# Query feature steps of four heads and 256 tokens in place of two heads and 512 tokens

## The reference

```python
def _fourier_kernel(x, proj_mat):
    p = jnp.einsum('blhd,dm->blhm', x, proj_mat) / math.sqrt(D_HEAD)
    return jnp.concatenate([jnp.cos(p), jnp.sin(p)], axis=-1) / math.sqrt(D_KMAP)
q = (x2 @ wq + bq).reshape(B, L, N_HEAD, D_HEAD)      # 16 heads of 16
k, v = ...                                            # the same with wk, wv
qp = _fourier_kernel(q, proj_mat)                     # 128 cosines, 128 sines a head
kp = _fourier_kernel(k, proj_mat)
kv = jnp.einsum('blhm,blhd->bhmd', kp, v)
attn = jnp.einsum('blhm,bhmd->blhd', qp, kv)
x = x + attn.reshape(B, L, D_MODEL) @ wo + bo
# then: layer norm, relu(x2 @ w1 + b1) @ w2 + b2 added
```

## Time and profile before

| | |
|---|---|
| median of three timed runs | 2267.7 us (2265.14 to 2273.48) |
| the profiled execution, its span from first to last instruction | 2298.2 us, 30.5 us (1.3%) over that median |
| mean granted TensorE clock | 0.942 of full speed |
| PE busy | 1940.0 us (84%) |
| DVE busy | 1682.0 us (73%) |
| ACT busy | 1255.4 us (55%) |
| POOL busy | 1225.0 us (53%) |
| query steps (qf) of batch 0, 1, 2, 3, from the first turns to the last attend's end | 98 to 154, 313 to 368, 527 to 581, 740 to 794 us |

### The profile page before, as it was taken

How to read it: one execution, slowest core, us unless ns; L and a number is a source line. 1 busy time by engine, 2 the same in 40 slices (tenths; PEclk the granted TensorE clock), 3 DMA queues, 4 the chain that set the end, 5 groups by cost and what they waited for, 6 DMA issues and landing times. The chain is left out here.

```text
span 2298.2 us, 25378 instructions
## 1 busy us (share of the span) xinstructions
PE 1940.0 (84%) x7956; PEld 1064.4 (46%) x7956; DVE 1682.0 (73%) x2212; ACT 1255.4 (55%) x1646; POOL 1225.0 (53%) x651
## 2 busy tenths in 40 slices
PE   5799889969987999889889888989876679989775
PEld 3346434643654354333334332533242238877664
DVE  4982787278548815799999999999989983325676
ACT  4862685278338723666654665466544435655443
POOL 3510621080126011488888999899967762214554
PEclk9899999989998999899999999999999899999887
DMA  6510550073035206688888899988899873224332
GB/s 193 118 30 1 169 125 1 29 191 74 1 99 139 75 0 72 204 292 290 283 315 303 272 285 309 307 284 282 291 319 371 313 253 104 97 90 119 119 118 70
DMA packets 177317, 402.61 MB, mean 175 GB/s; under 512 B 48174, under 2 KB 77104, under 8 KB 176034
## 3 DMA queue, kind: packets, MB, share of 16 engines
q1 hardware_dynamic: 165154, 371.09, 51.8%
q0 software_dynamic: 12032, 29.90, 4.4%
HBM read 356.30 MB, written 45.51 MB: 175 GB/s over the span
## 5 line engine op out<-in xcount | busy, mean ns | idle before, releaser
L1228 POOL TENSOR_TENSOR late<-late,rows 128x1024 f32<-128x1024 f32 x256 | 602.8, 2364 | 144.5 <-DVE late L1705 139.9
L1878 PE MATMUL m_Q<-late,ident_m 128*128 128x512 f32 x1024 | 529.5, 650 | 149.1 <-POOL late L1228 113.4
L1705 DVE TENSOR_TENSOR_SCAN late<-m_Q,late 128x1024 f32<-128x1024 f32 x256 | 586.2, 2290 | 39.9 <-ACT m_Q L1414 11.5
L1414 ACT ACTIVATE m_Q<-late,acol 128x1024 f32<-128x1024 f32 x256 | 286.1, 1117 | 361.0 <-DVE late L1705 358.8
L1878 PEld LDWEIGHTS m_Q<-late,ident_m 128*128 128x128 f32 x1024 | 196.4, 203 | 448.5 <-POOL late L1228 250.8
L1698 DVE TENSOR_TENSOR late<-m_Q,rows 128x1024 f32<-128x1024 f32 x256 | 307.0, 1199 | 13.6 <-DMA rows<-bc_s 13.4
L1937 PE MATMUL m_Q<-late 128*128 128x128 f32 x1248 | 167.4, 291 | 42.7 <-issue 36.2
L1937 PEld LDWEIGHTS m_Q<-late 128*128 128x128 f32 x1248 | 155.6, 203 | 68.9 <-issue 67.5
L492 DVE SCALAR_TENSOR_TENSOR early<-early,work 128x1024 f32<-128x1024 f32 x128 | 155.9, 1218 | 33.1 <-ACT early L628 30.9
L636 ACT ACTIVATE early<-early 128x1024 f32<-128x1024 f32 x128 | 134.8, 1053 | 42.7 <-DVE early L497 41.5
L313 POOL TENSOR_TENSOR qkh<-early,qkh 128x1024 bf16<-128x1024 f32 x12 | 25.5, 2127 | 245.6 <-ACT qkh L596 245.6
(11 more groups left out here) (234 smaller groups left out, 3349.6 us busy)
## 6 DMA issues: line engine op xcount, KB each, us to landing
rows<-bc_s SPq DMA_DIRECT2D x512, 512.0 KB, 5.5
rows<-st_s SPq DMA_DIRECT2D x64, 384.0 KB, 5.7
st_s<-qkh SPq DMA_DIRECT2D x16, 768.0 KB, 6.0
r_s<-late SPq DMA_DIRECT2D x39, 256.0 KB
rows<-st_s SPq DMA_DIRECT2D x64, 128.0 KB, 6.3
xin<-in_x SPq DMA_DIRECT2D x4, 1024.0 KB, 8.7
xres<-in_x SPq DMA_DIRECT2D x4, 1024.0 KB, 5.4
mx_s<-s SPq DMA_DIRECT2D x4, 1024.0 KB, 4.5
```

The source lines that it names most:

```text
L1228: nc.gpsimd.tensor_tensor(pr[:, n % NH, :], h[:, n % NH, :], cb[:, n % NCB, :], ALU.mult).then_inc(pr_ok, 1)
L1414: A(dA[:, :], dt[:, (b * KI + m) % 2, :], ACT.Exp, scale=acol[:, m, i % NS:i % NS + 1]).then_inc(dA_ok, 1)
L1705: v_.tensor_tensor_scan(h[:, n % NH, :], dA[:, :], dB[:, n % 2, :], 0.0, ALU.mult, ALU.add).then_inc(h_ok, 1)
L1878: ins = mm(half(Y, c), ident[:, :], half(pr[:, n % NH, :], c), start=False, stop=(n % NS == NS - 1), skip_group_check=True)
```

## The change

A query step holds four heads of one parity e (the even or the odd heads of a block of eight) over 256 tokens (TQ), where it held two heads over 512. Each of units 4 to 7 therefore loads every second head of its block. A unit's four steps go over the four quarters tq of the tokens; the two units of a block have e = 0 and e = 1. query_turns has four products of 256 columns. attend has eight products of 256 columns, over the four pairs a = 0 to 3, so that they go to four column groups and to half the columns (at) of the bank sums[c], c = tq // 2. The flag that starts a sum is given for the first quarter of a bank alone. The bank sums[0] is complete after the sixth and sums[1] after the eighth of eight steps. Steps, buffers, waits and the work of the other engines have the same number and size.

```diff
--- before.py
+++ after.py
@@ -17,6 +17,7 @@
 NT = B * TB
 KD = D // P
 CH = 512
+TQ = 256
 NC_ = L // CH
 EPS = 1e-5
 
@@ -246,7 +247,7 @@
                         sp.wait_ge(part_out[q % 2], (b * 2 + q // 2 + 1) * 16)
                     if u >= 2:
                         sp.wait_ge(rr_ok, b * 32 + 4 * (u - 2) + 4)
-                    heads = g["st_s"][u // 2, u % 2 * 4:u % 2 * 4 + 4]
+                    heads = g["st_s"][u // 2, u % 2 * 4:u % 2 * 4 + 4] if u < 4 else g["st_s"][u // 2, u % 2::2]
                     for p in (0, 3 * DH):
                         sp.dma_start(stack[p:p + 3 * DH, u % 2, :, :], heads.rearrange("h c s t -> (c s) h t")).then_inc(st_in[u % 2], 16)
                     for s in range(2):
@@ -774,12 +775,12 @@
 
                     def query_turns(s):
 
-                        u, c, e = 4 + s // 4, s // 2 % 2, s % 2
+                        u, tq = 4 + s // 4, s % 4
                         wait_slot(pe, b, "qf", s)
-                        if s % 4 == 0:
+                        if tq == 0:
                             pe.wait_ge(st_in[u % 2], (b * 4 + u // 2 + 1) * 64)
-                        for i in range(2):
-                            ins = mm(slot(b, "qf", s)[:, i * CH:(i + 1) * CH], projS[:, :], stack[:, u % 2, 2 * i + e, c * CH:(c + 1) * CH],
+                        for a in range(4):
+                            ins = mm(slot(b, "qf", s)[:, a * TQ:(a + 1) * TQ], projS[:, :], stack[:, u % 2, a, tq * TQ:(tq + 1) * TQ],
                                      start=True, stop=True)
                         done(ins, b, "qf", s)
 
@@ -809,17 +810,17 @@
                         ins.then_inc(kv_turned, 1)
 
                     def attend(s):
-                        mt, j, c, e = s // 8, s // 4 % 2, s // 2 % 2, s % 2
+                        mt, e, tq = s // 8, s // 4 % 2, s % 4
+                        c, at = tq // 2, tq % 2 * TQ
                         pe.wait_ge(feat_ok, b * 64 + 32 + 2 * s + 2)
                         if s in (0, 2):
                             pe.wait_ge(kv_ok, b * 8 + 6 + s)
                         if s in (8, 10):
                             pe.wait_ge(at_ok, b * 4 + (s - 6) // 2)
                         for cs, f in enumerate((fs, fc)):
-                            for i in range(2):
-                                a = 2 * j + i
-                                ins = mm(sums[c][32 * a:32 * a + 32, :], kv[:, mt * 4 + a, e, cs, :], f[:, (s + 16) % NF_, i * CH:(i + 1) * CH],
-                                         start=(e == 0 and cs == 0), stop=(e == 1 and cs == 1))
+                            for a in range(4):
+                                ins = mm(sums[c][32 * a:32 * a + 32, at:at + TQ], kv[:, mt * 4 + a, e, cs, :], f[:, (s + 16) % NF_, a * TQ:(a + 1) * TQ],
+                                         start=(e == 0 and cs == 0 and at == 0), stop=(e == 1 and cs == 1), skip_group_check=True)
                         return ins
 
                     def besides(s, second):
```

## The result

The changed kernel takes 2277.74 us (median of 16 runs, 2271.83 to 2283.42), the kernel before 2270.17 us (16 runs, 2264.86 to 2274.37). The ratio is 1.004, 95% interval [1.0031, 1.005]: slower by 0.4%, where +0.3% was forecast. In a later comparison (e7_after) it was 1.0034 [1.0021, 1.0047]. Two executions far above all others, one of e6_less_fill (2837.73 us) and one of the kernel before beside it (2902.04 us), both at a mean granted clock under 0.65, are in no ratio.

What follows compares the result with a forecast made beforehand. The query loop was taken as a chain of DVE and ACT, with PE on the path behind it. Per batch -0.2 - 0.3 + 2.0 = +1.5 us, times 4 = +6.0, giving 2273.6 us; range 2260 to 2283.

Steps and rivals of the forecast that it cites:

- The loop is a chain of DVE and ACT: Query steps 16 to 31: PE's time is covered by DVE and ACT, so the loop gains only 0.2 us a batch.
- attend like a key sum: One attend step: 16 matmuls in four column groups take 1.07 us, as the key sums do, in place of 1.91.
- query_turns and loads: Turns as four products of 256 columns, and loads of every second head: both cost 0, the loads staying hidden.
- The clock falls in the tail: Behind the last turns, PE works 3 x 1.07 us in 7.0, so the clock is 0.50 when wo starts.
- wo loses 1.7 to 2.8 us, 2.0 taken: Start of the products with wo: half rate loses 1.7 to 2.8 us a batch on the path; 2.0 taken.
- attend 31 gains in one batch of three, -0.3: Last attend, on the path: its 0.84 us gain is lost at half rate, counted in one batch of three, -0.3.
- Rival A: Tail of each batch: the clock stays up, -4.2 us in all, 2263.5 us; chance 0.20.
- Rival B: Half rate also reaches wkk's product before step 20's transposes, 1.88 becoming some 3.7 us; 2286 us; chance 0.10.
- Rival C: Query loop: PE's time does count, -16 us giving 2252, or -54 giving 2214; chance 0.05.
- D: Attends: four groups of this shape still run two at a time, PE stays full, time 2267.7 us; chance 0.05.

Runs made afterwards that it cites:

- e7_after: The changed kernel run a second time, unchanged, against the kernel before: ratio 1.0034 [1.0021, 1.0047].
- e6_less_fill: The changed kernel with about half the spare products (4, 1, 4 behind attends 28, 29, 30), against the kernel before: ratio 0.9983.
- e2: The changed kernel with two spare 128-column matmuls a batch, between attends 28 and 29 and between 30 and 31, against the kernel before: ratio 1.0042.
- e3: The new form in query steps 24 to 31 alone, the old form in steps 16 to 23, against the kernel before: ratio 1.0021.
- e5: The changed kernel with both products of a column group issued behind each other in attends 28 to 30, against the kernel before: ratio 1.0029.
- e1_fill: The changed kernel with spare 512-column products (7, 3, 7, 2) behind attends 28 to 31, results unused, against the kernel before: ratio 0.9978.
- e8_pairs: The changed kernel, attends 28 to 30 reordered by group, pairs 2 and 3 waiting until 0 and 1 finish, against the kernel before: ratio 0.9978.
- e9_more_fill: e1_fill plus the key turns of step 13 done five times over in batches 1 to 3, against the kernel before: ratio 0.9964.

## Why the prediction was right

The forecast (2273.6 us, +0.3%, in a range of 2260 to 2283) held, and so did its steps, with errors of size that are named here:

- *The loop is a chain of DVE and ACT: -0.2.* Measured from subtraction 16 to 31: -0.16, -0.25, -0.25, -0.24. In batch 1 the chain of step 22 gave 0.12 of the 0.15 read off it, and the 0.28 ahead was added to the wait at step 24, as said. The other 0.14, at step 21, the prediction had missed: it called PE late for one rounding alone, and PE was late for that of step 21 too.
- *attend like a key sum: 1.07.* Measured 1.07 at the full clock.
- *query_turns and loads: 0.* 0.61 us either way; no wait of PE for them appeared.
- *The clock falls in the tail.* It did in all four batches, and in all four of e7_after. The comparison with the key stretch in the earlier trace rows led to the right answer; that it is no sharp rule is seen in e6_less_fill, where the same work kept the clock in two batches and lost it in two.
- *wo loses 1.7 to 2.8 us, 2.0 taken.* Measured 1.46, 1.88, 1.71, 1.79, mean 1.7. The term was 0.3 too large: half rate outlasted wo's start by 3.0, 3.9, 3.5 and 3.6 us (in batch 1 from 369.91 to 373.8), at the lower of the two lengths that the prediction had read (3.4 and 5.6), and half of that is the loss.
- *attend 31 gains in one batch of three, -0.3.* It gained in none of the four here and none of the four of e7_after; in e2, e3 and e5 it did in five of twelve. The gain goes when the clock is down at the attend itself, and the loss at wo comes anyway.

The sum was +1.5 us a batch; the profile of the changed kernel gives -0.22 + 0.04 (the last attend and copy) + 1.70 = +1.5. That the two agree so well is in part luck: 0.3 too much at wo and 0.3 of gain at attend 31 that never came cancel. It makes 6.1 us of the 7.6 between the medians. The ratio's interval starts at 7.0 us, so 1 us or somewhat more isn't found in these stages. The traces put most of it ahead of them: PE's first product of the second phase starts at 895.42 us before and at 902.64 and 902.18 in the two profiles of the changed kernel, 7.2 and 6.8 later, and 1.8 and 0.9 of that is there already at the first subtraction of batch 0, ahead of every changed step. Why it is there stays open. Half-rate stretches in the key steps and in the second phase lie elsewhere in each profile, and no run here isolates them.

Rival A (-4.2 us, the clock stays up) is what e1_fill and e8_pairs made: -5.0 us by their ratios. Rival B did not happen: wkk's product of step 20 stayed at 1.88. Rival C is out: PE lost 11 us of work in the loop for 0.25. D is out by the 1.07.

The Trainium skill ("TensorE: Matmul & The Clock Gate", section "Why this matters for your kernels") warns of idle gaps between bursts. Read as a rule on single gaps it does not hold here: e2_ticks had none over 1.10 us in the tail of batch 1 and lost the clock; the kernel before, with one of 1.21, and e8_pairs, with one of 0.91 between longer attends, kept it.

## What to carry to other kernels

Before making PE faster in a stage that it doesn't bound, look at what PE does next: if dense products on the path follow a stretch that becomes loose, they start at half rate, and here that cost 1.7 us a batch against 0.25 won. In this tail, fast where it is on the path and slow where it is covered was the better form: only the last attend had to be short, and letting the three before it take 2.21 us (or adding spare products) turned +0.4% into -0.2%. The same can be tried wherever others wait for a product at half rate: in its one profile, e9_more_fill took 1.6 to 1.9 us out of the key steps of each of three batches with work that changes nothing.

## What the runs showed of the hardware

- Four column groups overlapped in both orders of issue: with the two products of one group behind each other an attend still took 1.09 us (e5_order), against 1.07 with the groups in turn. With a semaphore wait between two pairs of groups it took 2.21 us (e8_pairs).
- With one and the same program the clock at the same place was up in two batches and down in two (e6_less_fill). Half the spare work held it in two of four; the full spare work (e1_fill, e9_more_fill) and e8_pairs held it in four of four, each in one profiled execution.
- Half-rate stretches inside the query loop cost nothing: in e1_fill the clock falls to 0.50 once in the query steps of batches 2 and 3 and not in those of batch 1, and from subtraction 16 to 31 all three take 45.2 us. In batches 1 to 3 of e8_pairs it falls once too (353.9 to 357.4 in batch 1), and they take 45.2 us as well.
